# Start of a fused attention and deformable-convolution kernel: constants moved behind x on one queue, and a group-norm distance made on DVE

## The chip, the cores and the metric

One Trainium2 chip, one core. The metric is the device time of one execution in microseconds (us); the kernel before was run three times. Engines are called as the profile calls them: PE (TensorE matmuls), PEld (TensorE weight loads), DVE (VectorE), ACT (ScalarE), POOL (GpSimd) and SP (SyncE, which here only issues DMAs).

## What is computed

The input x is 8 images of 64 channels and 16 by 16 pixels, in fp32. Two layers follow each other, each on a group-normed copy of its input and each added back to that input:

```
x = x + L0(gn(x))     # 3x3 average pool, q/k/v/chans = pooled @ W_qkv, 3x3 local attention in 8 heads,
                      # out = out * gate(chans) + out, out @ Wp + bp
x = x + L1(gn(x))     # 3x3 conv makes offsets and masks, deformable 3x3 conv (4 groups), relu

def _gn(v, G=32, eps=1e-05):           # groups of 2 channels
    g = v.reshape(B_, G, C_ // G, H_, W_)
    m = jnp.mean(g, axis=(2, 3, 4)); s = jnp.var(g, axis=(2, 3, 4))
    return ((g - m) / jnp.sqrt(s + eps)).reshape(v.shape)
```

A group of the norm is a pair of channels. The kernel takes mean and variance of each channel by itself and joins them: the pair's variance is the mean of the two variances plus the square of one channel's distance to the pair's mean.

## The kernel before

The 128 partitions hold 64 channels of two halves of the batch; along a partition lie 4 images of 256 pixels (`N` = 1024 columns, two pieces of `BANK` = 512). The kernel is written engine by engine, with semaphores set by hand; each engine works through its own list in the order in which it is written.

At the start SP issues the loads: two pieces of x (L344, each 256 KB, semaphores `s_x[0]` and `s_x[1]`), then matrices of later stages (`bcast`, `womt`, `selx`, `sely`, `selm`) and small rows. ACT issues two loads of its own before it does anything else: `kept` (L495, 390.5 KB: the matrices `gnp`, `gnd` and `ident`, the taps `wfin`, the biases) and `attw` (L496, 480 KB: the attention's weights `wqkv`, `w1`, `w2`, `wp`, `headsum`, in the tile `vals_attw`).

The first norm and the pooled products then go like this:

- DVE waits for the first piece of x, makes statistics of its two images (`norm_stats`, L678 and L682, into `meanvar`) and starts its window sums (`window_sums(0, 0)`, L712 and L714). It waits for the second piece, makes its statistics, goes on with window sums (L716, L719) and then runs `norm(1)`.
- PE waits for `kept` and for all four images' statistics and runs `pair_stats(1)`: one matmul of `meanvar` with `gnp`, which gives the pair's means of mean and variance, and one with `gnd` (identity minus `gnp`), which gives each channel's distance to the pair's mean (L1015, L1016, both into bank 7).
- `norm(1)` copies bank 7 to `pair` (L688), squares the distance (L691) and adds square, variance and epsilon into `vareps` (L692). POOL raises that to the power -0.5 (`rstd`, L413). `link` in this code is an instruction followed by a wait for its own end.
- DVE normalises the pooled first piece (`pooled_norm(0)`, ending in L730, which counts `s_pool`), then finishes the window sums of the second piece and normalises that (L730 again).
- PE in the meantime runs three matmuls that rearrange `wfin` (L1030 to L1032; they need `by_tap`, an ACT copy out of `kept`), one product whose result nobody reads (`keep_warm(1)`, L1025), and then the q, k, v products (`qkv`, L1040): three of the first piece once `s_pool` is 1, two of the second once it is 2. The attention's logits (L1057) come next.

The same functions make the second norm, between the layers: `norm_stats` on `x2`, `keep_warm(2)`, `pair_stats(2)`, `keep_warm(3)` on PE, `norm(2)` on DVE, POOL's power (L446), then DVE normalises into the padded copy that the convolution reads (`normalise`, L695) and PE convolves (L1161). In the second layer a long loop over 72 taps runs PE, ACT, DVE and POOL together until the end.

Of the kernel before, what the change touches and what calls it, by code (L numbers as in the profile page):

```python
# [8 lines left out]
J = B // HALVES  # L9
P = HALVES * C  # L10
# [97 lines left out]
def bass_local_attention_then_deformable_conv(nc, x, cf, wom, sel16, rows16, out):  # L108
    fp32, bf16, fp16 = mybir.dt.float32, mybir.dt.bfloat16, mybir.dt.float16
    i32, u16 = mybir.dt.int32, mybir.dt.uint16  # L110
    ALU = mybir.AluOpType
# [5 lines left out]
    with ExitStack() as ctx:  # L117
        def sb(name, shape, dt=fp32):
            return ctx.enter_context(nc.sbuf_tensor(name, shape, dt))

        def sem(name):
            return ctx.enter_context(nc.semaphore(name))

        def views(words, *names):
# [5 lines left out]
            return out_  # L130

        kept = sb("kept", [P, sum(n for _, n in KEPT)])
        cst = views(kept, *KEPT)
        gnp, gnd, ident, bias = (cst[k] for k in ("gnp", "gnd", "ident", "bias"))
# [13 lines left out]
        minushalf = sb("minushalf", [P, J])  # L148
        halfstat = sb("halfstat", [P, 6 * J])
        meanvar = sb("meanvar", [P, 2 * J])  # L150
        pair = sb("pair", [P, 4 * J])
        gap2 = sb("gap2", [P, J])
        share = sb("share", [P, J])
        vareps = sb("vareps", [P, J])
# [4 lines left out]
        vals = sb("vals_attw", [P, 3 * 6 * C])  # L159
        cst.update(views(vals, *ATTENTION))  # L160
        attw = vals[:, 0:sum(n for _, n in ATTENTION)]

        conv_words = sb("conv_staged", [P, TAPSTEPS * OM + 2 * PAD])
# [42 lines left out]
        def bank(i, n=1):  # L206
            return ps[:, i * BANK:(i + n) * BANK]

        def images(t, w=HW):
            return t[:, :].rearrange("p (j n) -> p j n", j=J)  # L210
# [27 lines left out]
        def in_order(t, i):  # L238

            h, j = divmod(i, J)  # L240
            return t[:, (j * HALVES + h) * HW:(j * HALVES + h + 1) * HW]
# [5 lines left out]
        def sent(k, piece, i):  # L247

            n, lo, hi = piece
            row = "myx".index(k)  # L250
            return stack[k][i * ND:(i + 1) * ND, n * BANK + lo:n * BANK + hi], parts[row * ND:(row + 1) * ND, n % 2, i, lo:hi]

        def mask_columns(t, tap):

            return t[:, tap // 2 * P:(tap // 2 + 1) * P].rearrange("p (d e c) -> p e d c", d=DG, e=2)[:, tap % 2]
# [19 lines left out]
        s_cst, s_wom, s_sel, s_rows = sem("s_cst"), sem("s_wom"), sem("s_sel"), sem("s_rows")  # L275
        s_zero = sem("s_zero")
        s_bn = sem("s_bn")
        s_kept, s_bcast, s_byd, s_selxd, s_own = sem("s_kept"), sem("s_bcast"), sem("s_byd"), sem("s_selxd"), sem("s_own")
        s_perm, s_wtap, s_wzero, s_wfin = sem("s_perm"), sem("s_wtap"), sem("s_wzero"), sem("s_wfin")
        s_stats, s_pair, s_eps, s_rstd = sem("s_stats"), sem("s_pair"), sem("s_eps"), sem("s_rstd")  # L280
        s_counts = sem("s_counts")
# [59 lines left out]
        @block.sync  # L341
        def _(sp):
            for c in range(2):
                sp.dma_start(xin[:, c * BANK:(c + 1) * BANK], x[:, c * BANK:(c + 1) * BANK]).then_inc(s_x[c], 16)  # L344
            sp.dma_start(bcast[:, 2 * DG * P:], sel16["bcast"][:, 3 * DG * P:]).then_inc(s_bcast, 16)
            sp.dma_start(womt[:, :], wom).then_inc(s_wom, 16)
            sp.dma_start(selx[:, :].bitcast(u16), sel16["selx"]).then_inc(s_selxd, 16)
            sp.dma_start(bcast[:, 0:2 * DG * P], sel16["bcast"][:, DG * P:3 * DG * P]).then_inc(s_byd, 16)
            sp.dma_start(sely[:, :].bitcast(u16), sel16["sely"]).then_inc(s_sel, 16)
            for k in range(3):  # L350
                for a in range(2):
                    sp.dma_start(selm[:, k * P + a * C:k * P + (a + 1) * C].bitcast(u16).rearrange("p (d c) -> p d c", d=DG),
                                 mask_columns(sel16["selm"], 3 * a + k)).then_inc(s_sel, 16)
                sp.dma_start(selm[:, 3 * P + k * C:3 * P + (k + 1) * C].bitcast(u16).rearrange("p (d c) -> p d c", d=DG),
                             mask_columns(sel16["selm"], 6 + k)).then_inc(s_sel, 16)
            for k in "xym":
                sp.dma_start(stack[k][STACK:STACK + 2, :].bitcast(u16), rows16["x" if k == "x" else "y"]).then_inc(s_rows, 16)

            sp.wait_ge(s_x2, 2)
            for h in range(HALVES):  # L360
                sp.dma_start(x2seq[:, :].rearrange("c (j h n) -> c j h n", j=J, h=HALVES)[:, :, h, :],
                             images(x2)[h * C:(h + 1) * C]).then_inc(s_x2seq, 16)

            def odd_pairs(j):

                last = EVENS * (j + 1) - 1
                sp.wait_ge(s_xsa, last // 8 + 1)
                sp.wait_ge(s_xsd, (last // 4 + 1) // 2)
                to = (J * EVENS + j * ODDS) * P
                sp.dma_start(xs[0:C, to:to + ODDS * P], xs[C:P, j * EVENS * P:(j * EVENS + ODDS) * P]).then_inc(s_odd[j], 16)  # L370
                sp.dma_start(xs[C:P, to:to + ODDS * P], xs[0:C, (j * EVENS + 1) * P:EVENS * (j + 1) * P]).then_inc(s_odd[j], 16)

            for p, piece in enumerate(PIECES):
                for i in range(3):
                    sp.wait_ge(s_parts, 3 * p + i + 1)
                    sp.dma_start(*sent("y", piece, i)).then_inc(s_stack["y"][p], 16)
                for i in range(3):
                    if p:
                        sp.dma_start(*sent("x", piece, i)).then_inc(s_stack["x"][p], 16)
                for i in range(3):  # L380
                    if p:
                        whole = (piece[0], 0, BANK)
                        sp.dma_start(*sent("m", whole, i)).then_inc(s_stack["m"][p], 16)
                if p == 1:
                    odd_pairs(0)
                if p == 2:
                    for j in range(1, J):
                        odd_pairs(j)
            for i in range(B):
                sp.wait_ge(s_y, i + 1)  # L390
                sp.dma_start(in_order(out, i), result[:, i * HW:(i + 1) * HW]).then_inc(s_out, 16)
            sp.wait_ge(s_out, 16 * B)
            sp.wait_ge(s_choice, 1)
            passes = sp.value_load(choice[0:1, 0:1], min_val=1, max_val=SHIFTS)
            with sp.If(passes > 1):
                for i in range(B):
                    sp.wait_ge(s_y, B + i + 1)
                    sp.dma_start(in_order(out, i), result[:, i * HW:(i + 1) * HW]).then_inc(s_out, 16)
                sp.wait_ge(s_out, 2 * 16 * B)
# [92 lines left out]

        @block.scalar
        def _(act):
            act.dma_start(kept[:, :], cf[:, 0:kept.shape[1]]).then_inc(s_kept, 16)  # L495
            act.dma_start(attw, cf[:, kept.shape[1]:]).then_inc(s_cst, 16)  # L496

            act.wait_ge(s_kept, 16)
            act.wait_ge(s_zero, 4)

# [165 lines left out]
        def _(dve):  # L666
            chain = [0]

            def link(ins):

                chain[0] += 1
                ins.then_inc(s_dve, 1)
                dve.wait_ge(s_dve, chain[0])
# [10 lines left out]
            def norm(n):  # L684


                dve.wait_ge(s_pair, n)
                link(nc.vector.tensor_copy(pair[:, :], bank(7)[:, 0:4 * J]))  # L688
                gap = pair[:, 2 * J:4 * J].rearrange("p (j s) -> p j s", s=2)[:, :, 0]
                var = pair[:, 0:2 * J].rearrange("p (j s) -> p j s", s=2)[:, :, 1]  # L690
                link(nc.vector.tensor_tensor(gap2[:, :], gap, gap, ALU.mult))  # L691
                nc.vector.scalar_tensor_tensor(vareps[:, :], gap2[:, :], EPS, var, ALU.add, ALU.add).then_inc(s_eps, 1)  # L692

            def normalise(dst, src, j, rows=slice(0, P)):
# [45 lines left out]
            window_sums(0, 1)  # L740
            window_sums(0, 2)
            norm(1)
            window_sums(0, 3)
            window_sums(1, 0)
# [81 lines left out]
            for c in range(2):  # L826
                dve.wait_ge(s_x2, c + 1)
                norm_stats(x2, 2 * c)
            norm(2)
            dve.wait_ge(s_rstd, 2)  # L830

# [179 lines left out]
        def _(pe):  # L1011
            def pair_stats(n):

                pe.wait_ge(s_stats, n * J)
                nc.tensor.matmul(bank(7)[:, 0:2 * J], gnp, meanvar[:, :], start=True, stop=True)  # L1015
                nc.tensor.matmul(bank(7)[:, 2 * J:4 * J], gnd, meanvar[:, :], start=True, stop=True).then_inc(s_pair, 1)  # L1016

            def dense(dst, w, src, c, signal):
                nc.tensor.matmul(bank(dst + c), w, src[:, c * BANK:(c + 1) * BANK], start=True, stop=True).then_inc(signal, 1)
# [6 lines left out]

            pe.wait_ge(s_kept, 16)
            pair_stats(1)
            pe.wait_ge(s_perm, 1)
            nc.tensor.matmul(bank(1)[:, 0:PAIRS * C], by_tap[:, :], cst["wfin"], start=True, stop=True)  # L1030
# [89 lines left out]
            for c in range(2):  # L1120
                pe.wait_ge(s_hid, c + 1)
                nc.tensor.matmul(bank(3 - c), cst["w2"], hidden[:, c * BANK:(c + 1) * BANK], start=True,
                                 stop=True).then_inc(s_down, 1)
# [4 lines left out]
            for c in range(2):  # L1128
                rows = slice(c * C, (c + 1) * C)
                for t in range(TAPS):  # L1130
                    ins = nc.tensor.matmul(bank(3)[rows, 0:HF], cross[:, :], halves[c][:, t * HF:(t + 1) * HF], start=(t == 0),
                                           stop=(t == TAPS - 1))
# [414 lines left out]
```

## Time and profile before

| | |
|---|---|
| time of a run, median of 3 (lowest to highest) | 199.05 us (198.89 to 199.51) |
| profiled execution, first to last instruction (span) | 196.9 us |
| median above that span | 2.15 us |
| PE busy | 175.6 us (89%) |
| DVE busy | 158.0 us (80%) |
| ACT busy | 103.9 us (53%) |
| POOL busy | 86.3 us (44%) |
| share of PE, DVE, ACT in the chain that ended last | 69%, 13%, 7% |
| share of that chain spent on the load of x | 3% |

The profile gives the profiled execution's own time as its span; a run's time is taken over the whole launch, so the two differ by what lies around the span, here about 2.15 us. Busy shares are means over stages with different limits, so a change at the start is read at the start: which wait ends last there. The chain that ended last is followed back from the last instruction; it begins with the load of x. The clock column of the profile reads 1.00 (2.4 GHz) in every stretch of a few us.

### The profile page before, as it was taken

To read this page: it belongs to the slowest core of one execution; us is meant where nothing else is said; L and a number is where in the kernel's file an instruction comes from. 1 tells how busy PE (TensorE), PEld (TensorE's weight loads), DVE (VectorE), ACT (ScalarE), POOL (GpSimd) and SP (SyncE) were. 2 spreads that over 40 slices of the span, in tenths; PEclk is the share of its full clock that TensorE was granted. 3 is DMA by queue.
4 is the path that set the end of the run, shared out by engine and by line. 5 is a ranking of instruction groups with operands and counts; after the bars stand their busy time and mean duration, and the time that the engine had idled before them with its cause. 6 is when DMAs were issued, how large, how long until landed. Compare 5 with 4: busy or idle time off the path is not lost.

```text
span 196.9 us, 4523 instructions
## 1 busy us (share of the span) xinstructions
PE 175.6 (89%) x1774; PEld 123.8 (63%) x1774; DVE 158.0 (80%) x264; ACT 103.9 (53%) x195; POOL 86.3 (44%) x103
## 2 busy tenths in 40 slices
PE   0299996997979998999997999999889999999990
PEld 0224963653337545457686999648667788998880
DVE  0899958996559799984989998618999898999932
ACT  1136228610003795559856878537837868777000
POOL 8334983568020349504614527402733626636000
PEclk9999999999999999999999999999999999999998
DMA  6940000000040012216351000000012100000000
GB/s 187 346 39 3 3 0 0 3 0 0 0 107 3 26 35 49 82 33 153 86 123 52 4 3 0 3 0 0 12 30 59 28 3 17 3 17 2 20 0 22
DMA packets 9140, 7.65 MB, mean 39 GB/s; under 512 B 5015, under 2 KB 7589, under 8 KB 9113
## 3 DMA queue, kind: packets, MB, share of 16 engines
q1 hardware_dynamic: 8729, 6.35, 12.8%
q10 hardware_dynamic: 288, 0.89, 1.4%
q8 instruction: 16, 0.26, 0.6%
q14 instruction: 11, 0.09, 0.1%
q0 software_dynamic: 96, 0.06, 0.1%
HBM read 2.82 MB, written 0.52 MB: 17 GB/s over the span
## 4 chain that ended last, share of the span: by engine, by line
PE 69%; DVE 13%; ACT 7%; issue 4%; DMA 3%; POOL 1%; SPq 0%; DVEq 0%
PE ps L1267 19%; PE ps L1241 11%; PE ps L1161 10%; PE ps L1057 4%; DVE smp_prod L790 3%; DMA x_parts<-in_x 3%; PE ps L1226 3%; PE ps L1094 3%; PE ps L1309 3%; PE ps L1315 3%; PE ps L1040 3%; PE ps L1025 2%; DVE smp_prod L901 2%; PE ps L1212 2%; PE ps L1178 2%
## 5 line engine op out<-in xcount | busy, mean ns | idle before, releaser
L901 DVE TENSOR_TENSOR smp_prod<-ps,hx_selx 128x768 f32<-128x768 f32 x72 | 67.0, 952 | 7.3 <-PE ps L1241 6.3
L1267 PE MATMUL ps<-smp_prod,windows_attention 128*64 128x192 f32 (+2 forms) x512 | 54.5, 336 | 0.1
L1267 PEld LDWEIGHTS ps<-smp_prod,windows_attention 128*64 128x64 f32 x512 | 38.9, 136 | 5.1 <-DVE windows_attention L886 0.4
L1241 PE MATMUL ps<-haty,by_rows 128*64 128x256 f16 x432 | 38.8, 274 | 2.4 <-DVE smp_prod L901 2.2
L465 POOL TENSOR_SCALAR disty<-disty 64x512 f32<-64x512 f32 (+1 forms) x23 | 12.8, 557 | 58.8 <-ACT haty L610 58.7
L1241 PEld LDWEIGHTS ps<-haty,by_rows 128*64 128x64 f16 x432 | 26.5, 109 | 7.5 <-DVE smp_prod L901 3.9
L618 ACT ACTIVATE hx_selx<-ps 128x512 f32<-128x512 f32 x36 | 21.3, 592 | 16.5 <-PE ps L1226 16.5
L472 POOL TENSOR_TENSOR haty<-disty,haty 64x512 f16<-64x512 f32 (+1 forms) x23 | 24.0, 1046 | 1.9
L1161 PE MATMUL ps<-conv_staged 128*108 128x512 f32 (+1 forms) x60 | 23.3, 521 | 0.7 <-ACT x_parts L582 0.6
L620 ACT ACTIVATE hx_selx<-hx_selx 128x512 f32<-128x512 f32 x36 | 22.7, 631 | 1.1
L915 DVE TENSOR_TENSOR vals_attw<-ps,windows_attention 128x384 f32<-128x384 f32 x24 | 13.3, 553 | 5.8 <-PE ps L1267 3.2
L605 ACT ACTIVATE disty<-ps 128x512 f32<-128x512 f32 (+1 forms) x24 | 12.5, 520 | 8.8 <-PE ps L1212 8.1
L468 POOL TENSOR_SCALAR disty<-disty 64x512 f32<-64x512 f32 (+1 forms) x23 | 15.7, 684 | 1.9
L1226 PE MATMUL ps<-stack_x,selx 110*64 110x256 bf16 x144 | 15.9, 272 | 0.0
L1161 PEld LDWEIGHTS ps<-conv_staged 128*108 128x108 f32 x60 | 9.5, 172 | 8.1 <-issue 5.8
L610 ACT ACTIVATE haty<-disty 128x512 f16<-128x512 f32 (+1 forms) x24 | 13.4, 559 | 0.8
L596 ACT COPY windows_attention<-ps 128x512 f32<-128x512 f32 (+1 forms) x24 | 11.2, 468 | 4.7 <-PE ps L1195 2.7
L582 ACT ACTIVATE x_parts<-ps,kept 108x256 f32<-108x256 f32 (+1 forms) x3 | 1.6, 540 | 22.1 <-PE ps L1161 22.1
L436 POOL TENSOR_TENSOR smp_prod<-smp_prod 128x1024 f32<-128x1024 f32 x4 | 9.4, 2361 | 6.0 <-DVE smp_prod L790 6.0
L1094 PE MATMUL ps<-smp_prod,kept 128*128 128x512 f32 x20 | 9.6, 611 | 1.6 <-POOL smp_prod L436 1.6
L790 DVE TENSOR_TENSOR smp_prod<-ps,windows_attention 128x1024 f32<-128x1024 f32 x9 | 10.5, 1212 | 0.1
L1226 PEld LDWEIGHTS ps<-stack_x,selx 110*64 110x64 bf16 x144 | 9.9, 110 | 0.0
(140 smaller groups left out, 262.5 us busy)
## 6 DMA issues: line engine op xcount, KB each, us to landing
windows_attention<-windows_attention SPq DMA_DIRECT2D x8, 256.0 KB, 3.8
x_parts<-in_x SPq DMA_DIRECT2D x2, 256.0 KB, 5.3
bcast<-in_bcast SPq DMA_DIRECT2D x2, 256.0 KB, 6.6
x2seq<-x_parts SPq DMA_DIRECT2D x2, 256.0 KB, 3.8
out<-x_parts SPq DMA_DIRECT2D x8, 64.0 KB, 2.3
vals_attw<-in_cf ACTq DMA_DIRECT2D x1, 480.0 KB, 5.9
stack_m<-x_parts SPq DMA_DIRECT2D x12, 36.0 KB
kept<-in_cf ACTq DMA_DIRECT2D x1, 390.5 KB, 4.4
```

Of the source, the lines that this page charges most:

```text
L468: nc.gpsimd.tensor_scalar(d, d, -1.0, 1.0, ALU.add, ALU.mult).then_inc(s_uy, 1)
L472: nc.gpsimd.tensor_tensor(hi, d, hi, ALU.add).then_inc(s_loy, 1)
L610: nc.scalar.activation(haty[i % 2][:, YP[e] * HW:YP[e] * HW + w], d, ACT.Relu, bias=1.0, scale=-1.0).then_inc(s_hiy, 1)
L618: nc.scalar.activation(h, bank(5), ACT.Abs).then_inc(s_absx, 1)
L620: nc.scalar.activation(h, h, ACT.Relu, bias=1.0, scale=-1.0).then_inc(s_hatx, 1)
L790: nc.vector.tensor_tensor(grid(prod[:, t * N:(t + 1) * N]), grid(bank(PB[pos % 3], 2)), shifted(vpad, t), ALU.mult).then_inc(s_pv, 1)
L901: nc.vector.tensor_tensor(pairs, rows, cols.unsqueeze(1).to_broadcast([P, QUARTERS, HW]), ALU.mult).then_inc(s_mult, 1)
L1094: ins = nc.tensor.matmul(bank(2 + c), ident, prod[:, t * N + c * BANK:][:, 0:BANK], start=(t == 0), stop=(t == 6))
L1161: ins = nc.tensor.matmul(bank(CONV_BANK[p])[0:OM, lo:hi], womt[:, k * OM:(k + 1) * OM], shifted(dup[h], 3 * ky + 2 * single)[:, j:j + (hi ...
L1226: ins = nc.tensor.matmul(bank(5)[h * C:(h + 1) * C, k * HW:(k + 1) * HW], selx[:, tap * P + h * C:tap * P + (h + 1) * C], stack["x"][:, i ...
L1241: ins = nc.tensor.matmul(ps[h * C:(h + 1) * C, at:at + HW], by_matrix(a, QUARTERS - 1 - k)[:, h * C:(h + 1) * C], haty[i % 2][:, p * HW:(p ...
L1267: return nc.tensor.matmul(dst[:, at:at + strips * 3 * SP].rearrange("p (s k n) -> p s k n", k=3, n=SP), rows, sampled(i, ki, m, first, str ...
```

## The change

Two edits. The two loads that ACT issued are now issued by SP, behind the two pieces of x and ahead of everything else. And the distance to the pair's mean is no longer a matmul with `gnd`: DVE subtracts the channel's own mean from the pair's mean in bank 7, and copies half as many columns to `pair`. Since the squared distance is what is used, its sign does not matter. The copy now has a semaphore of its own (`s_paircopied`), for which `vareps` waits. The matrix `gnd` is still loaded as part of `kept`. Both norms use the changed functions.

```
@@ sync
             for c in range(2):
                 sp.dma_start(xin[:, c * BANK:(c + 1) * BANK], x[:, c * BANK:(c + 1) * BANK]).then_inc(s_x[c], 16)
+            sp.dma_start(kept[:, :], cf[:, 0:kept.shape[1]]).then_inc(s_kept, 16)
+            sp.dma_start(attw, cf[:, kept.shape[1]:]).then_inc(s_cst, 16)
             sp.dma_start(bcast[:, 2 * DG * P:], sel16["bcast"][:, 3 * DG * P:]).then_inc(s_bcast, 16)
@@ scalar
-            act.dma_start(kept[:, :], cf[:, 0:kept.shape[1]]).then_inc(s_kept, 16)
-            act.dma_start(attw, cf[:, kept.shape[1]:]).then_inc(s_cst, 16)
@@ vector, norm(n)
                 dve.wait_ge(s_pair, n)
-                link(nc.vector.tensor_copy(pair[:, :], bank(7)[:, 0:4 * J]))
-                gap = pair[:, 2 * J:4 * J].rearrange("p (j s) -> p j s", s=2)[:, :, 0]
+                own_mean = meanvar[:, :].rearrange("p (j s) -> p j s", s=2)[:, :, 0]
+                mean = bank(7)[:, 0:2 * J].rearrange("p (j s) -> p j s", s=2)[:, :, 0]
+                gap = pair[:, 2 * J:3 * J]
                 var = pair[:, 0:2 * J].rearrange("p (j s) -> p j s", s=2)[:, :, 1]
+                link(nc.vector.tensor_tensor(gap, mean, own_mean, ALU.subtract))
+                nc.vector.tensor_copy(pair[:, 0:2 * J], bank(7)[:, 0:2 * J]).then_inc(s_paircopied, 1)
                 link(nc.vector.tensor_tensor(gap2[:, :], gap, gap, ALU.mult))
+                dve.wait_ge(s_paircopied, n)
                 nc.vector.scalar_tensor_tensor(vareps[:, :], gap2[:, :], EPS, var, ALU.add, ALU.add).then_inc(s_eps, 1)
@@ tensor, pair_stats(n)
                 pe.wait_ge(s_stats, n * J)
-                nc.tensor.matmul(bank(7)[:, 0:2 * J], gnp, meanvar[:, :], start=True, stop=True)
-                nc.tensor.matmul(bank(7)[:, 2 * J:4 * J], gnd, meanvar[:, :], start=True, stop=True).then_inc(s_pair, 1)
+                nc.tensor.matmul(bank(7)[:, 0:2 * J], gnp, meanvar[:, :], start=True, stop=True).then_inc(s_pair, 1)
```

SP's list at the very start of the program, before the change (`x_parts` is the tile of x, `in_` names are the inputs in device memory, `conv_staged` holds `womt`):

```order
L344 DMA x_parts<-in_x 128x512 x2
L345 DMA bcast<-in_bcast 128x1024
L346 DMA conv_staged<-in_wom 128x648
L347 DMA selx<-in_selx 110x1152
L348 DMA bcast<-in_bcast 128x1024
L349 DMA s_sely<-in_sely 110x640
```

The same place after the change:

```order
L344 DMA x_parts<-in_x 128x512 x2
L345 DMA kept<-in_cf 128x781
L346 DMA vals_attw<-in_cf 128x960
L347 DMA bcast<-in_bcast 128x1024
L348 DMA conv_staged<-in_wom 128x648
L349 DMA selx<-in_selx 110x1152
L350 DMA bcast<-in_bcast 128x1024
L351 DMA s_sely<-in_sely 110x640
```

The two loads from `in_cf` stand third and fourth; everything behind them keeps its order, two issues later. ACT's list begins with its first copy (L501 before), without issues ahead of it.

DVE's list at the first norm, before the change, with the semaphores that each waits for (`gap` is the tile of `gap2`):

```order
L716 TENSOR_TENSOR windows_attention<-windows_attention,x_parts 128x2x16x14
L719 TENSOR_TENSOR windows_attention<-windows_attention 128x512 [waits s_counts,s_dve]
L688 COPY pair<-ps 128x16 [waits s_pair,s_dve]
L691 TENSOR_TENSOR gap<-pair 128x4 [waits s_dve]
L692 SCALAR_TENSOR_TENSOR vareps<-gap,pair 128x4 [waits s_dve]
L721 TENSOR_TENSOR windows_attention<-windows_attention 128x512
```

And after it:

```order
L719 TENSOR_TENSOR windows_attention<-windows_attention,x_parts 128x2x16x14
L722 TENSOR_TENSOR windows_attention<-windows_attention 128x512 [waits s_counts,s_dve]
L691 TENSOR_TENSOR pair<-ps,meanvar 128x4 [waits s_pair,s_dve]
L692 COPY pair<-ps 128x8 [waits s_dve]
L693 TENSOR_TENSOR gap<-pair 128x4
L695 SCALAR_TENSOR_TENSOR vareps<-gap,pair 128x4 [waits s_paircopied,s_dve]
L724 TENSOR_TENSOR windows_attention<-windows_attention 128x512
```

One small instruction has been added between the window sums: four in place of three, still with two waits of DVE for itself behind the one for PE. The square no longer waits for the copy. On PE only the row of L1016 has gone.

## Rows read from the trace of the kernel before

**Rows 1.** The chain that ended last, first 20 us: start us, us, what.

```profile
0.74 0.41 SPq L344
...
1.22 5.99 DMA x_parts<-in_x
...
8.49 0.56 PE ps L1015 x2
9.05 0.43 PE ps L1016 x2
...
14.02 3.14 PE ps L1040 x6
...
17.18 1.98 PE ps L1040 x4
```

**Rows 2.** Timeline, first 20 us: start us, us, engine line op, last what ended idleness.

```profile
5.36 0.75 DVE L678 BATCH_NORM_STATS2 halfstat<-x_parts 128x6 f32<-128x256 f32 x2 [4.18 <-DMA x_parts<-in_x]
5.44 0.30 ACT L501 COPY by_tap<-kept 128x128 f32<-128x128 f32 x1
...
6.41 0.65 DVE L714 TENSOR_TENSOR windows_attention<-x_parts 128x480 f32<-128x480 f32 x1
7.30 0.75 DVE L678 BATCH_NORM_STATS2 halfstat<-x_parts 128x6 f32<-128x256 f32 x2 [0.24 <-DMA x_parts<-in_x]
...
8.88 0.69 DVE L719 TENSOR_TENSOR windows_attention<-windows_attention 128x512 f32<-128x512 f32 x1
...
9.61 0.17 DVE L688 COPY pair<-ps 128x16 f32<-128x16 f32 x1
...
10.02 0.16 DVE L692 SCALAR_TENSOR_TENSOR vareps<-gap,pair 128x4 f32<-128x4 f32 x1
10.10 0.68 DVE L721 TENSOR_TENSOR windows_attention<-windows_attention 128x512 f32<-128x512 f32 x1
...
12.69 0.88 DVE L730 SCALAR_TENSOR_TENSOR windows_attention<-windows_attention,rstd 128x256 f32<-128x256 f32 x2
...
16.25 0.88 DVE L730 SCALAR_TENSOR_TENSOR windows_attention<-windows_attention,rstd 128x256 f32<-128x256 f32 x2
```

**Rows 3.** DMA issues by line: queue, KB each, median us from issue to landing.

```profile
out<-x_parts SPq DMA_DIRECT2D x8, 64.0 KB, 2.3
vals_attw<-in_cf ACTq DMA_DIRECT2D x1, 480.0 KB, 5.9
...
kept<-in_cf ACTq DMA_DIRECT2D x1, 390.5 KB, 4.4
```

**Rows 4.** Landing of L361, two transfers of 256 KB back to back on SP.

```profile
DMA to landing us min/median/max: 3.5/3.8/4.0
```

**Rows 5.** Windows of the start: busy us of each engine, PEclk, DMA share, GB/s.

```profile
0.00:3.00 3.00, 0.00 (x0) 0.00 (x0) 0.33 (x4) 0.00 (x0) 2.46 (x8) 1.00 0.38 79
3.00:5.00 2.00, 0.00 (x0) 0.00 (x0) 0.00 (x0) 0.85 (x1) 2.00 (x3) 1.00 1.01 358
7.00:8.00 1.00, 0.00 (x0) 0.00 (x0) 0.76 (x3) 0.00 (x0) 0.00 (x0) 1.00 1.05 407
```

**Rows 6.** Timeline of the second norm, 56 to 60 us.

```profile
56.15 0.39 PE L1015 MATMUL ps<-meanvar,kept 128*128 128x8 f32 x2 [0.99 <-DVE meanvar L682]
...
56.40 0.37 PE L1016 MATMUL ps<-meanvar,kept 128*128 128x8 f32 x2
...
56.62 2.82 PE L1025 MATMUL ps<-kept 128*128 128x512 f32 x6
56.80 0.17 DVE L688 COPY pair<-ps 128x16 f32<-128x16 f32 x1 [0.70 <-PE ps L1016]
...
58.51 3.42 DVE L695 TENSOR_SCALAR conv_staged<-x_parts,pair,rstd 64x256 f32<-64x256 f32 x8 [1.14 <-POOL rstd L446]
...
59.49 7.98 PE L1161 MATMUL ps<-conv_staged 128*108 128x256 f32 x30
```

**Rows 7.** Line L1025, both keep_warm places: ns min/median/max, first and last start.

```profile
L1025 PE MATMUL ps<-kept x12: 593/593/1222, 11.9 to 58.8; 128*128 128x512 f32 x12
```

More of the change, by code:

```diff
@@ L150, in bass_local_attention_then_deformable_conv @@
         meanvar = sb("meanvar", [P, 2 * J])
-        pair = sb("pair", [P, 4 * J])
+        pair = sb("pair", [P, 3 * J])
         gap2 = sb("gap2", [P, J])
@@ L277, in bass_local_attention_then_deformable_conv @@
         s_bn = sem("s_bn")
-        s_kept, s_bcast, s_byd, s_selxd, s_own = sem("s_kept"), sem("s_bcast"), sem("s_byd"), sem("s_selxd"), sem("s_own")
+        s_kept, s_paircopied, s_bcast, s_byd, s_selxd, s_own = sem("s_kept"), sem("s_paircopied"), sem("s_bcast"), sem("s_byd"), sem("s_selxd"), sem("s_own")
         s_perm, s_wtap, s_wzero, s_wfin = sem("s_perm"), sem("s_wtap"), sem("s_wzero"), sem("s_wfin")
```

## The prediction

> **What bounds the kernel now.** I read the chain that ended last first, because 199 us of mostly PE work says little about an edit at the start. Its first piece is a wait: it issues x at 0.74, sits on the landing of x's second piece until 7.21, and PE's first matmul of the norm stands at 8.49 [rows 1]. From there to the logits the chain runs on PE, so one might take PE for the limit. The timeline shows a second line of work that is just as late. DVE starts at 5.36 when piece 0 lands, is through with its window sums at 7.06 (6.41 + 0.65), waits 0.24 us for piece 1, and from 7.30 has almost no gap until its second L730 ends at 17.13 (16.25 + 0.88) [rows 2]. The first six passes of L1040 end on PE at 17.16 (14.02 + 3.14), and the four of the second piece start at 17.18 [rows 1]. So PE and DVE arrive within 0.03 us of each other, and whatever is gained there must be gained on both. Behind 17.18 I find no time that is fixed from outside: nothing on SP's list behind `attw` is read before the first six L1040 passes, so later work moves with that start.
>
> **Edit 1, the loads.** Before, SP's and ACT's loads were in flight together. ACT's `kept`, issued with x at the program's start, landed 4.4 us after its issue, at about 5.14 [rows 3], while piece 0, issued at 0.74, was there at 5.36 [rows 1, 2]: 0.66 MB came in together (262 KB and 400 KB), and piece 0 waited for bytes that no one needs before 8.49. Bytes moved are 79 GB/s x 3 us = 0.24 MB at 3.0, and 358 GB/s after that [rows 5]. By that curve 0.66 MB were through at 4.18, 1.0 to 1.2 us before the two landings; I take 1.05 us from last byte to landing. For the new order, estimates by the same curve:
> - piece 0 (0.262 MB): through at 3.06, lands about 4.1;
> - piece 1 (0.524 MB): 3.8, lands about 4.85;
> - `kept` (0.924 MB): 4.9, lands about 5.95;
> - `attw` (1.415 MB): 6.3, lands about 7.3; that is about what it takes now, 5.9 us from an issue behind `kept`'s on ACT [rows 3].
>
> A second reading of piece 0: the nearest transfer of its size, 256 KB first of two on SP's queue with nothing else in flight, lands 3.5 us after issue [rows 4], which gives 4.24. I take 4.2. Then DVE's first stretch of 1.70 us ends at 5.9; piece 1 is there by then; the 0.24 us wait goes too. With 0.04 us of turn-round the statistics of piece 1 start at 5.95 instead of 7.30: **1.35 us earlier**. PE wants `kept` 1.19 us after that point (8.49 - 7.30), at 7.15, and it lands at 5.95, so its later landing is covered by 1.2 us. ACT's `by_tap` copy, 0.30 us [rows 2], then ends near 6.3; its reader comes behind the pair matmul, after 7.15: covered. `attw` is wanted by L1040 past 12: covered by 5 us. If either cover is gone, each us of lateness costs a us. The loads behind shift by two issues, some 0.9 us by 0.41 us of issue and a gap each [rows 1]; their readers come after the logits begin, cost nothing. ACT loses two issues ahead of work for which it waits anyway: nothing.
>
> The Trainium skill, page "DMA: Bandwidth & Descriptors", section "Anatomy of one DMA — SWDGE (gpsimd) path", puts one DMA at about 2.0 us fixed plus bytes at 436 GB/s. By that, an estimate, piece 0 would land 2.6 us after its issue, at 3.34, and the sum would be about 0.9 us better. The 3.5 us of a transfer of that very size here [rows 4] speaks against it (and the page's fit is for another issuing path), so the row decides.
>
> **Edit 2, first norm.** PE loses L1016, 0.43 us [rows 1]. But DVE does not wait for it: L719 ends at 9.57 and the copy follows at 9.61 [rows 2], which is only its turn-round. With one matmul the sum would be ready 0.43 us before DVE can take it, so the saving is on PE alone. DVE gets a fourth small instruction. Not waited for, one of these costs what L692 to L721 shows, 0.08 us; with a wait behind it, half of the 0.41 us from L688 to L692, 0.20 us [rows 2]. The new copy is not waited for at once, so I take 0.1. DVE's line thus gains 1.35 - 0.1 = **1.25 us**, and PE's line 1.35 + 0.43 = 1.78. PE's fake product then ends at 14.02 - 1.78 = 12.24, and the first L730 at 13.57 - 1.25 = 12.32: DVE decides when L1040 starts. Its second L730 ends at 15.88 and PE must have made six passes by then. A pass at 2.4 GHz is 0.45 us ((2.82 - 0.59) / 5) [rows 6, 7], and one of the L1040 passes before ran slower: 3.14 - 5 x 0.45 leaves 0.9, and L1025 shows 1222 ns beside 593 [rows 7], the lower level (1.2 GHz) by its duration, though the clock column reads 1.00. Before, PE reached full speed about 14.9, 6.4 us after its first matmul. If that moves along with the first matmul (to 13.5), L1040 has 1.2 us at 0.9 a pass, then 4.7 passes at 0.45: done at 15.6, before DVE. So DVE's 1.25 us stand.
>
> **Edit 2, second norm.** Here DVE does wait: its copy at 56.80 follows the end of L1016 at 56.77; L1015 ended at 56.54 [rows 6]. The sum is ready 0.23 earlier, the extra instruction takes 0.1: vareps, POOL's power and L695 come 0.13 earlier. The convolution starts at 59.49, when keep_warm ends at 59.44 and two L695 (0.86 of 3.42) end at 59.37 [rows 6]. PE's own line moves by the same 0.22. Either way 0.13 to 0.22; I take 0.13. Bounds: 0.02 (an instruction at 0.20) to 0.22.
>
> **Sum.** 1.35 - 0.1 + 0.13 = 1.38 us. The span goes from 196.9 to 195.5, and with 2.15 us around it the time to 199.05 - 1.38 = **197.7**. Edit 2 by itself is close to nothing (-0.1 + 0.13). Bounds of the landing of piece 0: unchanged 5.36 leaves only the 0.24 us wait, 198.8; 64 KB out to memory in 2.3 us [rows 3] plus 0.2 MB more at 358 GB/s (0.55) gives 2.85 us, landing at 3.6 and 0.6 better, 197.1.
>
> **The rivals.**
> - *The load is quicker still.* The landing at 3.6 just worked out: piece 1 would be there at about 4.3, before 5.3 where DVE takes it; 197.1. The page's rule above goes this way and further (196.8). For it: a store with nothing beside it lands in 2.3. Against it: rows 4.
> - *A latency hidden either way.* If piece 0's 4.6 us are mostly start-up of cold queues and not shared bandwidth, DVE starts where it did and gains the 0.24 us wait only: 199.05 - 0.24 - 0.03 = 198.8, no change that can be measured. For it: only 0.24 MB moved in the first 3 us. Against it: 358 GB/s follow at once, shared by two queues.
> - *The clock stays where it was.* The Trainium skill, page "TensorE: Matmul & The Clock Gate", Part 1, says that the number of slow matmuls at the start differs from run to run, because the moment of the rise has nothing to do with the program's start. As a mechanism here: full speed still at 14.9, L1040 from 12.35: 2.8 passes at 0.9, 3.2 at 0.45, done at 16.3 instead of 15.9. That eats 0.4 us: 198.1.
> - *`kept` becomes the wait, and it gets slower.* PE's pair matmul waits for both. Third on one queue, `kept` may land until 7.6, since DVE takes the pair matmul's result no earlier than 8.2; past that a us costs a us. The whole gain is gone at about 9.0, and the time is 0.6 us worse than before at 9.6. For that 0.924 MB would have to come at some 0.14 MB/us from 2 us on. Against it: between 7 and 8 us, with ACT's loads landed, SP's queue by itself moved 407 GB/s [rows 5]. Partly true (landing at 8.2) it gives 198.3.
>
> **How the numbers follow.** A difference of 0.3% (0.6 us) is about what a measurement of this kernel can tell from no change. Chances: forecast (197.2 to 198.1) 0.65; quicker load 0.1; clock 0.1; latency hidden 0.09; `kept` late 0.06, half of it slower than before. Faster by over 0.3% (under 198.45): 0.65 + 0.1 + 0.1 and a little of the last = 0.86. Within 0.3%: 0.09 and what is left, 0.11. Slower: 0.03. The range runs from the quicker load to just short of the hidden latency, 196.9 to 198.6.
>
> **What the changed profile would show.** Piece 0's statistics near 4.2 and not 5.4, piece 1's at 5.9 to 6.0 with no DMA wait ahead of them; the pair matmul near 7.15, released by `meanvar` and not by `kept`; DVE's first instruction of the norm right behind L719 (now L722), some 0.5 us after PE's result; L1040 released by DVE's L730 (now L733) at 12.3 and 15.9; in the second norm 0.13 us between the two gains. Beyond the logits every group should keep its busy time. The prediction is wrong if the first statistics do not move, if PE's first matmul waits for a DMA, or if an early gain is given back before the convolution.

## The result and the profile after

The changed kernel takes 197.26 us in the median of 4 executions (197.17 to 197.83). The kernel before, beside it, takes 198.97 (4 executions, 198.45 to 199.51). The ratio is 0.9915 [0.9891, 0.994]: 1.7 us less. The profiled execution of the changed kernel has a span of 195.2 us against 196.9.

The chain that ended last in the first 20 us of the changed kernel (start us, us, what) begins like this:

```profile
0.74 2.80 DMA x_parts<-in_x
3.54 0.03 issue
3.57 0.76 DVE halfstat L677 x2
```

Piece 0 of x landed at 3.54, 2.80 us after its issue; before, DVE's first statistics stood at 5.36 [rows 2]. The wait for piece 1, 5.99 us of [rows 1], is gone from the chain: from 3.57 on it is DVE's own work. The timeline of the changed kernel (start us, us, engine, line, what, and in brackets the idle time before it with its releaser) shows the first norm:

```profile
3.57 0.75 DVE L677 BATCH_NORM_STATS2 halfstat<-x_parts 128x6 f32<-128x256 f32 x2 [2.38 <-DMA x_parts<-in_x]
5.30 0.75 DVE L677 BATCH_NORM_STATS2 halfstat<-x_parts 128x6 f32<-128x256 f32 x2
...
6.09 0.25 DVE L681 BATCH_NORM_AGGREGATE meanvar<-halfstat 128x2 f32<-128x6 f32 x2
...
6.53 0.30 ACT L500 COPY by_tap<-kept 128x128 f32<-128x128 f32 x1 [1.10 <-DMA kept<-in_cf]
6.55 0.60 PE L1018 MATMUL ps<-meanvar,kept 128*128 128x8 f32 x2 [6.55 <-DMA kept<-in_cf]
6.88 0.69 DVE L722 TENSOR_TENSOR windows_attention<-windows_attention 128x512 f32<-128x512 f32 x1
7.61 0.16 DVE L691 TENSOR_TENSOR pair<-ps,meanvar 128x4 f32<-128x4 f32 x1
7.80 0.17 DVE L692 COPY pair<-ps 128x8 f32<-128x8 f32 x1
7.88 0.15 DVE L693 TENSOR_TENSOR gap<-pair 128x4 f32<-128x4 f32 x1
8.07 0.16 DVE L695 SCALAR_TENSOR_TENSOR vareps<-gap,pair 128x4 f32<-128x4 f32 x1
8.15 0.69 DVE L724 TENSOR_TENSOR windows_attention<-windows_attention 128x512 f32<-128x512 f32 x1
```

Three things are to be read here against [rows 2]. Piece 1's statistics start at 5.30 instead of 7.30 with no DMA ahead of them: 2.00 us earlier, of which 1.79 is piece 0's landing and 0.21 the wait for piece 1. PE's pair matmul is released by the DMA of `kept`, at 6.55, and not by the statistics, whose second L681 ends at 6.34 (6.09 + 0.25); so the cover that `kept` was to have is used up, though DVE takes the result only behind its L722, at 7.61, and loses nothing. And from DVE's first instruction of the norm to the next window sum are 0.54 us (7.61 to 8.15) where there were 0.49 (9.61 to 10.10): the extra instruction costs 0.05.

The same view of PE and DVE up to the second piece of q, k and v:

```profile
9.61 1.90 PE L1027 MATMUL ps<-kept 128*128 128x512 f32 x2
11.78 2.81 PE L1042 MATMUL ps<-windows_attention,vals_attw 128*128 128x512 f32 x6 [0.27 <-DVE windows_attention L733]
14.30 0.88 DVE L733 SCALAR_TENSOR_TENSOR windows_attention<-windows_attention,rstd 128x256 f32<-128x256 f32 x2
15.23 1.98 PE L1042 MATMUL ps<-windows_attention,vals_attw 128*128 128x512 f32 x4 [0.65 <-DVE windows_attention L733]
```

PE now waits for DVE at both places. The second part starts at 15.23 instead of 17.18 [rows 1], 1.95 earlier, and this lead is unchanged through the attention: in the second norm (same view) the pair matmul stands at 54.20 instead of 56.15 [rows 6].

```profile
54.20 0.39 PE L1018 MATMUL ps<-meanvar,kept 128*128 128x8 f32 x2 [0.99 <-DVE meanvar L681]
54.63 0.16 DVE L691 TENSOR_TENSOR pair<-ps,meanvar 128x4 f32<-128x4 f32 x1 [0.48 <-PE ps L1018]
56.40 3.41 DVE L698 TENSOR_SCALAR conv_staged<-x_parts,pair,rstd 64x256 f32<-64x256 f32 x8 [1.14 <-POOL rstd L448]
57.38 2.81 PE L1163 MATMUL ps<-conv_staged 128*108 128x256 f32 x12
```

DVE's normalising starts at 56.40 instead of 58.51, the convolution at 57.38 instead of 59.49: the lead has grown by 0.16 to 2.11. It stays there until one DVE instruction of the sampling loop (the long loop of the second layer), which starts late with no releaser for the last part of its wait. Timeline of before, then of the changed kernel:

```profile
99.28 0.36 ACT L596 COPY windows_attention<-ps 128x256 f32<-128x256 f32 x1
99.73 0.56 DVE L915 TENSOR_TENSOR vals_attw<-ps,windows_attention 128x384 f32<-128x384 f32 x1 [0.74 <-ACT windows_attention L596]
```

```profile
97.16 0.35 ACT L595 COPY windows_attention<-ps 128x256 f32<-128x256 f32 x1
97.97 0.56 DVE L918 TENSOR_TENSOR vals_attw<-ps,windows_attention 128x384 f32<-128x384 f32 x1 [1.09 <-ACT windows_attention L595]
```

ACT's copy comes 2.12 us earlier, the product that reads it only 1.76: it starts 0.46 us after the copy's end where before it was 0.09. The chain of the changed kernel (start us, us, what) puts that time down to nothing that the profile knows:

```profile
97.16 0.36 ACT windows_attention L595
97.52 0.03 issue
97.55 0.02 DVEq L322
97.57 0.40 issue
97.97 0.09 DVE vals_attw L918
```

DVE's queue has been let go at 97.57 and the instruction starts 0.40 us later. From there to the end the lead is 1.7 us. The balance: 2.00 (loads) - 0.05 (first norm) + 0.16 (second norm) - 0.34 (this delay) = 1.77.

### The profile page after: what moved, and what is told of

It is laid out like the page before. It is cut to its first block, busy times and chain, and to the rows that moved or that the text cites. A ratio compares the mean times of both kernels' runs of the same rounds, so it can differ in the third digit from the quotient of the medians.

```text
span 195.2 us, 4519 instructions
## 1 busy us (share of the span) xinstructions
PE 174.5 (89%) x1770; PEld 122.8 (63%) x1770; DVE 157.8 (81%) x266; ACT 103.8 (53%) x195; POOL 86.5 (44%) x103
## 3 DMA queue, kind: packets, MB, share of 16 engines
q1 hardware_dynamic: 9017, 7.24, 14.5%
## 4 chain that ended last, share of the span: by engine, by line
PE 63%; DVE 18%; ACT 8%; issue 5%; POOL 2%; DMA 1%; DVEq 0%; POOLq 0%
PE ps L1269 19%; PE ps L1243 10%; PE ps L1163 10%; PE ps L1059 4%; DVE smp_prod L793 3%; PE ps L1228 3%; PE ps L1096 3%; PE ps L1311 3%; PE ps L1317 3%; DVE smp_prod L904 2%; PE ps L1214 2%; ACT disty L604 2%; PE ps L1180 2%; ACT haty L609 1%; DVE halfstat L677 1%
## 6 DMA issues: line engine op xcount, KB each, us to landing
kept<-in_cf SPq DMA_DIRECT2D x1, 390.5 KB, 4.8
```

## The experiments

**The loads alone.** The old norm with the two load lines moved:

```
@@ sync, behind the two pieces of x
+            sp.dma_start(kept[:, :], cf[:, 0:kept.shape[1]]).then_inc(s_kept, 16)
+            sp.dma_start(attw, cf[:, kept.shape[1]:]).then_inc(s_cst, 16)
@@ scalar
-            act.dma_start(kept[:, :], cf[:, 0:kept.shape[1]]).then_inc(s_kept, 16)
-            act.dma_start(attw, cf[:, kept.shape[1]:]).then_inc(s_cst, 16)
```

> Only the loads are moved; the norm is that of the kernel before (two matmuls, one copy of 16 columns). Theory (x's bytes waited for kept's and attw's bytes, and that is the whole gain): statistics of x's first piece at 3.5 to 3.7 us as in the changed kernel, second L730 ends at 15.1 to 15.2, second norm 0.16 us longer than in the changed kernel, time 197.2 to 197.6. Rival (the new norm has a good part of the gain): 198.0 or more.

197.23 us, ratio 0.990 [0.9879, 0.992]: the whole gain, as expected. The rival that the norm's edit carries a good part of it falls. The profile is of the slowest of four executions (197.83); its second L729 ends at 15.89 and not at 15.1 to 15.2, and it shows how thin the cover of `kept` is. Timeline:

```profile
3.46 0.76 DVE L677 BATCH_NORM_STATS2 halfstat<-x_parts 128x6 f32<-128x256 f32 x2 [2.28 <-DMA x_parts<-in_x]
5.20 0.75 DVE L677 BATCH_NORM_STATS2 halfstat<-x_parts 128x6 f32<-128x256 f32 x2
7.24 0.60 PE L1014 MATMUL ps<-meanvar,kept 128*128 128x8 f32 x2 [7.24 <-DMA kept<-in_cf]
7.69 0.57 PE L1015 MATMUL ps<-meanvar,kept 128*128 128x8 f32 x2
8.37 0.17 DVE L687 COPY pair<-ps 128x16 f32<-128x16 f32 x1 [0.90 <-PE ps L1015]
```

Here `kept` came at 7.2, and DVE idled 0.90 us for PE.

**The norm alone.** The loads as before, the new `norm` and `pair_stats`:

```
@@ vector, norm(n)
+                link(nc.vector.tensor_tensor(gap, mean, own_mean, ALU.subtract))
+                nc.vector.tensor_copy(pair[:, 0:2 * J], bank(7)[:, 0:2 * J]).then_inc(s_paircopied, 1)
...
@@ tensor, pair_stats(n)
-                nc.tensor.matmul(bank(7)[:, 2 * J:4 * J], gnd, meanvar[:, :], start=True, stop=True).then_inc(s_pair, 1)
```

> Only the norm is changed; ACT issues the two loads as before. Theory: first statistics at 5.36 as before, DVE takes PE's result no earlier than before because of the window sums and loses 0.05 us, the second norm gains 0.16 us; 198.7 to 199.1. Rival (the new norm has a good part of the gain): 198.2 or less.

199.30 us, ratio 1.0006 [0.9995, 1.0018]: no gain, as the theory says, but the time lies 0.2 us above the range it gave. The range had no term for the delayed instruction, which is there too:

```profile
9.59 0.16 DVE L692 TENSOR_TENSOR pair<-ps,meanvar 128x4 f32<-128x4 f32 x1
...
99.99 0.56 DVE L919 TENSOR_TENSOR vals_attw<-ps,windows_attention 128x384 f32<-128x384 f32 x1 [1.09 <-ACT windows_attention L596]
```

DVE takes PE's result at 9.59 where it did at 9.61 [rows 2], though one matmul less stands ahead of it. In the loop it idles 1.09 us, as in the changed kernel, and the product stands 0.26 us later than before (99.99 against 99.73): the 0.35 of the delay less the 0.1 that the two norms gain together.

**How much may travel beside x.** Two kernels on the changed one put a part of the constants back on ACT's queue at the program's start: 64 KB (the matrix `gnp`, with a semaphore of its own), and the 480 KB of `attw`.

```
@@ scalar, 64 KB                                   @@ scalar, 480 KB
+ act.dma_start(kept[:, 0:P], cf[:, 0:P])...       + act.dma_start(attw, cf[:, kept.shape[1]:])...
@@ sync                                            @@ sync
- sp.dma_start(kept[:, :], ...)                    - sp.dma_start(attw, ...)
+ sp.dma_start(kept[:, P:], ...)
@@ tensor
+ pe.wait_ge(s_gnp, 16) ahead of pair_stats(1)
```

> The changed kernel, but ACT issues the 64 KB of gnp at the start, with a semaphore of its own for which the first pair matmul waits; the other 326.5 KB of kept and attw stay behind x on SP. Theory (bytes beside x delay x in proportion): first statistics later by 64 KB at 358 GB/s, 0.2 us, so at 3.7 to 3.9; pair matmul released by the statistics; 197.3 to 197.6. Rival (any load on ACT's queue ahead of or beside x's costs x its start, whatever its size): first statistics at 4.8 or later, 198.3 or more.

> The changed kernel, but ACT issues attw (480 KB) at the start and only kept stands behind x on SP. Theory (shared bandwidth, engines taking turns between the queues): piece 0 lands as late as before or later, first statistics at 5.3 to 5.6, because 480 KB lie beside it where 390.5 KB did; kept lands at 7 to 7.7; 198.7 to 199.2. Rival (it was kept being ahead of x, not bytes beside it): first statistics below 4.5, 197.5 or less.

64 KB: 197.72 us, ratio 0.9928 [0.9909, 0.9948]. 480 KB: 199.13 us, ratio 1.0003 [0.9991, 1.0014], the whole gain gone. DVE's first statistics in the timeline, with 64 KB, then with 480 KB:

```profile
4.00 0.75 DVE L679 BATCH_NORM_STATS2 halfstat<-x_parts 128x6 f32<-128x256 f32 x2 [2.83 <-DMA x_parts<-in_x]
```

```profile
5.40 0.75 DVE L678 BATCH_NORM_STATS2 halfstat<-x_parts 128x6 f32<-128x256 f32 x2 [4.22 <-DMA x_parts<-in_x]
```

| beside x at the start | piece 0's statistics start at |
|---|---|
| nothing (changed, loads alone) | 3.57, 3.46 us |
| 64 KB | 4.00 |
| 390.5 KB, with 480 KB behind it (before) | 5.36 |
| 480 KB | 5.40 |

What lies beside x sets its landing. The rival that a second queue costs the same whatever its size (4.8 or later) falls with the 64 KB, and the rival that only `kept` being ahead of x mattered falls with the 480 KB of another load. But the theory's "in proportion" is not borne out either. The 64 KB cost 0.4 to 0.5 us, where their bytes alone were to cost 0.2: the statistics (expected at 3.7 to 3.9) and the time (197.3 to 197.6) both missed their ranges on the late side. And 480 KB delayed the statistics only 0.04 us more than 390.5 KB with 480 KB behind it. How much of the 64 KB's cost is bytes and how much the second queue as such, no run separates.

**The loads back on ACT, but held back.** If only the first microseconds count, ACT may issue both loads itself once an early semaphore of another engine has come, here at 1.83 us:

```
+            act.wait_ge(s_zero, 1)
+            act.dma_start(kept...); act.dma_start(attw...)     # instead of SP's two
```

> The changed kernel, but ACT issues both loads as before, held back until POOL's first memset is done (about 1.8 us), so that x has a head start though the queue is another. Theory (bytes in flight beside x count, not the queue's name): first piece untouched, its statistics at 3.5 to 3.9 us; piece 1 shares with kept and lands up to 1 us later, its statistics at 5.2 to 5.8; kept lands by 6.3; 197.1 to 197.8. Rival (only one queue's order gives x the lead): first statistics at 4.5 or later, 198.2 or more.

A miss: 199.10 us, ratio 0.9997 [0.9977, 1.0017]. The timeline shows x unhurt (3.44 and 5.18, where piece 1 was expected up to 1 us later) and a new wait:

```profile
1.83 0.38 ACTq L496 DMA_DIRECT2D kept<-in_cf  x1
...
3.44 0.75 DVE L679 BATCH_NORM_STATS2 halfstat<-x_parts 128x6 f32<-128x256 f32 x2 [2.27 <-DMA x_parts<-in_x]
...
8.94 0.60 PE L1020 MATMUL ps<-meanvar,kept 128*128 128x8 f32 x2 [8.94 <-DMA kept<-in_cf]
```

`kept` now runs beside the matrices that SP issues behind x. Its group in the DMA issues (engine, operation, count, KB each, median us from issue to landing), then the same of the changed kernel:

```profile
kept<-in_cf ACTq DMA_DIRECT2D x1, 390.5 KB, 7.1
```

```profile
vals_attw<-in_cf SPq DMA_DIRECT2D x1, 480.0 KB, 6.3
...
kept<-in_cf SPq DMA_DIRECT2D x1, 390.5 KB, 4.8
```

So the order on one queue seems to do two things: it keeps `kept` away from x, and it keeps the later matrices back behind `kept`. The first is what the table shows. The second is argued: by 8.0 us this kernel had moved 1.80 MB (its windows from 0 to 3, 5, 7 and 8 us show 105, 216, 329 and 396 GB/s), about twice the 0.92 MB of x and `kept`, and `kept` was still not there; no run holds the later matrices back as well. Either way the prediction's rival "`kept` becomes the wait" comes true here: PE starts at 8.94, later than the 8.49 of before, and all is lost. This run's own rival, that only the order of one queue gives x its lead, falls by the statistics at 3.44 (4.5 or later was its sign): x kept its lead with loads of another queue issued 1.1 us behind it.

**The delayed instruction.** The norm's edit puts one instruction and one wait more into DVE's list in each of the two norms, four entries in all. To see whether the delay belongs to the norm or to a place in the list, four one-column memsets of a tile that nothing reads are put into DVE's list behind the second pooled norm (they run at 15.58 us in the first of these three kernels), long before the delayed product: on the changed kernel, on the loads alone with the old norm, and on the norm alone.

```
+            for n in range(4):
+                nc.vector.memset(spare[:, n:n + 1], 0.0)
```

> The changed kernel with four one-column memsets on DVE ahead of the logits, where DVE has slack; nothing reads them. In the changed kernel one DVE product at 97.97 us starts 0.42 us after its last wait is over, where it was 0.06 before, and all later work shifts with it; every kernel with the new norm shows it. Theory (the place of that instruction in DVE's list causes it; the new norm only added entries ahead of it): the product starts within 0.1 us of its wait, the gain of 0.35 us stays: 196.8 to 197.0. Rival (something in the new norm's work or in memory causes it): delay still there, 197.2 to 197.4.

> Only the loads are moved (old norm, as in the run with the loads alone), plus the same four memsets on DVE. Theory of the place in the list: the delay of 0.35 us appears before the same product though the norm is the old one; 0.35 us longer than without the memsets, when kept lands at the same time: 197.4 to 197.9. Rival (the new norm causes it): no delay there, time as with the loads alone, 197.0 to 197.4.

> Only the norm is changed (loads as before), plus DVE's four memsets. Theory (the new norm by itself is worth 0.05 us lost and 0.16 won; the delay of 0.35 us in DVE's list is what made it slower by 0.1): no delay before the product at 99.7, 198.9 to 199.15, below the run without the memsets by 0.2 to 0.35. Rival (the norm costs something of its own later): 199.2 or more.

The product in question in the timelines, first on the changed kernel, then with the old norm, then on the norm alone:

```profile
97.83 0.56 DVE L921 TENSOR_TENSOR vals_attw<-ps,windows_attention 128x384 f32<-128x384 f32 x1 [0.74 <-ACT windows_attention L596]
```

```profile
98.08 0.56 DVE L917 TENSOR_TENSOR vals_attw<-ps,windows_attention 128x384 f32<-128x384 f32 x1 [1.09 <-ACT windows_attention L596]
```

```profile
99.84 0.56 DVE L922 TENSOR_TENSOR vals_attw<-ps,windows_attention 128x384 f32<-128x384 f32 x1 [0.74 <-ACT windows_attention L597]
```

| kernel | entries more on DVE than before | idle before the product | time, ratio |
|---|---|---|---|
| before | 0 | 0.74 us | |
| loads alone | 0 | 0.74 | 197.23, 0.990 [0.9879, 0.992] |
| norm alone | 4 | 1.09 | 199.30, 1.0006 [0.9995, 1.0018] |
| changed | 4 | 1.09 | 197.26, 0.9915 [0.9891, 0.994] |
| loads alone + 4 | 4 | 1.09 | 197.94, 0.9943 [0.9922, 0.9964] |
| norm alone + 4 | 8 | 0.74 | 198.99, 0.9998 [0.9988, 1.0008] |
| changed + 4 | 8 | 0.74 | 197.02, 0.9894 [0.9865, 0.9923] |

The delay goes with the number of entries and not with the norm: with four more it is there, with none or eight it is not. The other kernels agree: those with 64 KB, with 480 KB and with the loads held back have four entries more and idle 1.08 to 1.09 us there, and the two with `gnp` first, below, have eight and idle 0.74. The times are a blunter measure. By the two ratios, loads alone lose 0.4%, some 0.9 us, by the four memsets, over twice the delay, and the single executions with them run from 197.31 to 198.65; what the rest is, the profile, of the fastest of them, does not show. The last row has the lowest median but one of all kernels, yet its interval overlaps with that of the changed kernel. With the delay gone the norm's edit is still worth nothing that the times show (0.9998).

**`gnp` ahead of the rest of `kept`.** To take the DMA wait from PE's pair matmul, SP issues the 64 KB of `gnp` first, then `kept` without the now unread `gnd`; the fake product reads other columns, and the four memsets stay.

```
-            sp.dma_start(kept[:, :], ...)
+            sp.dma_start(kept[:, 0:P], ...).then_inc(s_gnp, 16)
+            sp.dma_start(kept[:, 2 * P:], ...).then_inc(s_kept, 16)
@@ tensor
-            pe.wait_ge(s_kept, 16); pair_stats(1)
+            pe.wait_ge(s_gnp, 16); pair_stats(1); pe.wait_ge(s_kept, 16)
```

> The changed kernel; SP issues the 64 KB of gnp by itself right behind x, then the rest of kept without gnd (262.5 KB), then attw; the first pair matmul waits for gnp alone; the fake products read other columns of kept; and the four memsets on DVE. Theory (kept is at the edge of deciding the first pair matmul, in the profile of the loads alone it decided by 0.8 us): pair matmul released by the statistics at 6.4 to 6.6; with the delay on DVE also gone 196.6 to 197.0. Rival (one more issue and a small transfer cost as much as they save): as with the memsets alone or slower.

196.93 us, ratio 0.9894 [0.9864, 0.9924]: within the range of the theory, but no better than the changed kernel with four memsets (197.02), as its rival has it. The timeline tells why:

```profile
6.49 0.56 PE L1022 MATMUL ps<-meanvar,kept 128*128 128x8 f32 x2 [6.49 <-DVE meanvar L683]
...
7.76 0.30 ACT L502 COPY by_tap<-kept 128x128 f32<-128x128 f32 x1 [2.33 <-DMA kept<-in_cf]
8.20 1.40 PE L1037 MATMUL ps<-kept,by_tap 128*128 128x320 f32 x2 [1.14 <-ACT by_tap L502]
...
12.67 4.82 PE L1047 MATMUL ps<-windows_attention,vals_attw 128*128 128x512 f32 x10
```

The pair matmul is released by the statistics, as meant, but the rest of `kept` came at 7.7, and PE stood idle 1.14 us for `by_tap`. PE reached q, k and v at 12.67 and not at 11.78 as in the changed kernel. That left the fake product `keep_warm(1)` as work on the path, so the next kernel is the same without it (its result is read by nobody):

```
-            keep_warm(1)
```

> The kernel with gnp first and DVE's four memsets, without the first fake product of PE (keep_warm(1)). In its predecessor the late rest of kept moved to by_tap (copy at 7.76 us) and through PE's rearranging matmuls and the fake product to the first q, k, v product at 12.67, half a us past the sums that DVE had ready by 11.64. Theory (PE's list is what is late there): the first q, k, v product starts by 11.8, DVE's logit products at 15.5, 0.3 us better than its predecessor: 196.4 to 196.8. Rival (the fake product pays for itself by the clock): q, k, v passes run at 1.2 GHz past 12, six passes end after 15.5: 196.9 or more.

A miss, and the rival (the fake product pays for itself by the clock) came true: 198.34 us where 196.4 to 196.8 was expected, ratio 0.9959 [0.9942, 0.9976], by the two ratios 0.65% of the time before, 1.3 us, worse than with it. PE's q, k, v products in the groups from 8 to 30 us (count, busy us, mean ns of one, idle before), of the kernel without the fake product and of the changed kernel:

```profile
L1046 PE MATMUL ps<-windows_attention,vals_attw 128*128 128x512 f32 x16 | 9.8, 767 | 1.1 <-DVE windows_attention L735 1.1
```

```profile
L1042 PE MATMUL ps<-windows_attention,vals_attw 128*128 128x512 f32 x16 | 7.6, 610 | 0.9 <-DVE windows_attention L733 0.9
```

The timeline of the kernel without it:

```profile
11.76 6.93 PE L1046 MATMUL ps<-windows_attention,vals_attw 128*128 128x512 f32 x10 [1.09 <-DVE windows_attention L735]
```

PE started at 11.76, 0.9 us earlier than with the fake product, but ten products took 6.93 us where 4.82 did. By their durations (up to 1193 ns, with a median of 592) the first of them ran at the lower of the two levels (1.2 GHz); the clock column reads 1.00 in both.

## Why the prediction was right, and where its sizes were off

**What bounds the start.** Right. PE and DVE both had to gain, and both did; the gain is DVE's, as in the sum, since L1042 waits for DVE's L733 at 11.78 and at 15.23.

**Edit 1, the landing of piece 0.** The mechanism was right, the size was off: the term 1.35 us measured 2.00. The failing step is the landing "I take 4.2", drawn from the 3.5 us of [rows 4] and from the curve of [rows 5]; it was 3.54, within 0.1 us of the rival "quicker still" (3.6), which is what happened; "a latency hidden either way" fell with it. The row of 3.5 us was no like for like: L361 copies from one tile to another (`x2seq<-x_parts`, 64 partitions) and loads nothing from device memory. The windows (start:end, length, busy PE, PEld, DVE, ACT and POOL, clock, DMA share, GB/s) show why the curve did not carry over:

```profile
0.00:3.00 3.00, 0.00 (x0) 0.00 (x0) 0.33 (x4) 0.00 (x0) 2.46 (x8) 1.00 0.35 113
3.00:5.00 2.00, 0.00 (x0) 0.00 (x0) 1.40 (x6) 0.86 (x1) 2.00 (x3) 1.00 0.96 259
```

By 3.0 us 0.34 MB had moved on one queue, where two queues had moved 0.24 [rows 5]; the curve of two queues at once was too slow a measure for one. After that it was too fast a one: 259 GB/s and not 358. The Trainium skill, page "DMA: Bandwidth & Descriptors", section "Anatomy of one DMA — SWDGE (gpsimd) path", gave as an estimate 2.6 us from issue to landing, which I set aside for the row of 3.5; the 2.80 measured agrees better with the page, although its fit is for another issuing path.

**Edit 1, `kept`.** "Covered by 1.2 us" failed. It landed at about 6.5 instead of 5.95, because of the lower rate after 3 us, and was wanted at 6.5 instead of 7.15, because all else was earlier. The prediction had named "PE's first matmul waits for a DMA" as a sign that it is wrong, and on this point the sign came: the pair matmul stood at 6.55, released by `kept`, and not near 7.15, released by `meanvar`. The wait is 0.06 us in this profile and hidden behind L722, but in that of the loads alone it was 0.85 (7.24 against 5.20 + 1.19, the time from piece 1's statistics to PE's start in [rows 2, 1]). The kernel with the loads held back lost everything by it. The chance of 0.06 for this rival was low for a cover that thin.

**Edit 2, first norm.** Right: the saved matmul stays on PE (DVE at 9.59 against 9.61 with the norm alone), and the extra DVE instruction costs 0.05 where I took 0.1. **Second norm.** Right: 0.16, where I took 0.13 out of 0.02 to 0.22.

**The clock.** The rival that full speed stays at 14.9 us fell: the six products from 11.78 took 2.81 us, 0.47 each, so it was there before 11.78. It did not merely move along with the first matmul either (6.55 to 11.78 is at most 5.2 us, where I had read 6.4). Nor does the distance hold from run to run: with the loads alone and four memsets the first matmul stood at 6.48, and the six products, from 12.03 on, took 3.15 us, with one of 1089 ns, so the lower level was still there after 12. It cost next to nothing: those six products ended at 15.18, and DVE's second L730, for which the second part waits too, at 15.12.

**"I find no time that is fixed from outside."** Not so simple: 0.34 us are given back at 97.97, by a mechanism that the prediction does not name. It took half of what the load was better than forecast, so the forecast came nearer than its terms deserve: 1.38 forecast, 1.77 by the profile, of which the load is +0.65, the two norms +0.08, the delay -0.34. That the time came within the band of the forecast, 197.2 to 198.1, is luck: with the delay gone (the changed kernel with four memsets) it is 197.02.

## What to carry to other kernels

A load that the first work waits for should come first, with no load issued beside it on another queue: 64 KB beside the 256 KB cost 0.4 to 0.5 us here, 390.5 KB 1.8. Loads issued behind it do not have to wait until it has landed: here five were issued by then on the same queue, and in one run two on another. Next, look for the load that becomes last when the first one is quicker, and keep the later loads behind that one as well, as the order on one queue did here. Taking an instruction from an engine for which nobody waits bought nothing here, and a shift of a few entries in an engine's list can by itself move a later instruction by some tenths of a us (0.35 here), so small effects need a control with the same number of entries.

## What was not expected of the hardware

One DVE product starts 0.35 us later when its list is longer by four entries, and on time with none or eight more, in all twelve kernels. It waits for no semaphore and no DMA that the trace shows. That instructions are fetched late at this place would fit, but it is only argued. The nearest 8 KB packet of an instruction queue (q14) does move with the list: it starts 2.2 us behind the product's start with no entry more (two kernels), 1.7 us behind with four (six) and 2.6 to 2.9 us ahead with eight (four). But no trace shows whose instructions it carries, or that the product waits for it. The cause is open.

Two queues at the start moved less in the first 3 us than one did (0.24 MB against 0.34; in all profiles 0.20 to 0.25 MB with 390.5 or 480 KB beside x, and 0.29 to 0.35 with nothing beside it). And `kept`, third on one queue, was what released PE's pair matmul in four profiles, at 6.48, 6.55, 7.10 and 7.24 us, with the same loads ahead of it; what makes it vary by nearly 0.8 us the runs do not tell.
